# Attention over eight images: both output groups at the start of a pass, back to back

## The chip, the cores and the metric

The kernel runs on 1 core of one Trainium2 chip. The metric is device time in microseconds (us) of one execution. The engines are named as the profile names them: PE (TensorE, with PEld for its weight loads), DVE (VectorE), ACT (ScalarE), POOL (GpSimd) and SP (SyncE, which here issues DMAs).

## What is computed

The input x has 8 images of 768 channels and 32 x 32 = 1024 positions. It is normalised in 32 groups, goes through 12-head attention with head size 64, and is added back:

```python
def _L0_conv_ref(x, Wq, Wk, Wv, Wp):
    ...
    q = conv1x1(Wq)
    k = conv1x1(Wk)
    v = conv1x1(Wv)
    scale = 1.0 / jnp.sqrt(jnp.asarray(dh, dtype=x.dtype))
    scores = jnp.einsum('bhdn,bhdm->bhnm', q, k) * scale
    attn = jax.nn.softmax(scores, axis=-1)
    out = jnp.einsum('bhnm,bhdm->bhdn', attn, v)
    out = out.reshape(B, C, H, W)
    return jnp.einsum('oc,bchw->bohw', Wp, out)
...
x = x + _L0_conv_ref(_gn(x), L0_conv_Wq, L0_conv_Wk, L0_conv_Wv, L0_conv_Wp)
```

## The kernel before

A first phase (`project_phase`, about the first 1220 us) normalises x and writes q, k and v to DRAM. The change does not touch it. The second phase (`attend_phase`) is a chain of 48 **passes**, 0 to 47, one for each pair of heads: 6 passes make one image. Every engine runs its own program in order, and they meet only at semaphores, so the order in which each program is written out is the schedule.

A pass has 8 **steps** t (128 keys each). PE does in a step:

- `scores_by_key` (L873): the scores of pass p, 128 keys by 1024 queries for two heads, in two halves h. Each half is 8 matmuls in two PSUM banks. The first 6 are q times k, the last 2 (shown as `ones_r`) subtract each query's maximum, which lies in a row `top`. ACT turns each half into exponents (L988, tile `p_all`, a ring of three slots).
- `scores_by_query` (L855), called a **unit**: scores of the next pass, laid out so that DVE can take maxima (L1026). There are 16 units in a pass and one pair of banks for them, so a unit waits for the maximum of the unit before it.
- `values` (L886): exponents times v, for the step before. `values` of step 7 is done in the next pass.
- An **out group** (`output`, L896): 18 matmuls of the last projection for an earlier image, 128 channels by 512 positions, from tile `a`. From pass 8 on (`LAG` = 8) each pass has two, numbered 0 and 1; both write PSUM bank 7, and DVE adds x to the result (`add_x`, L1065).

The bank of an out group is also one of the banks of scores (`SCORE_BANKS = (0, 1, 2, 7)`, where the last two are half h = 1). So half 1 of a step waits for the `add_x` behind a group.

At the end of a pass DVE turns the maxima into rows (L93, L97, L99), and SP sends them with two DMAs to `top` (L87). POOL adds the exponents up over the steps (L830, 14 adds a pass), multiplies the heads of pass p - 2 by their reciprocal sums in step 1 (`divide`, L813), and in step 3 makes their low part (`low_out`, L818). SP stores the high and low parts to DRAM (L743, L745).

Tile `a` holds 6 blocks of those heads for half an image. SP **reloads** it in every third pass (10, 13, ..., 46, thirteen times): after the store of the low part has landed it issues six DMAs of 512 KB (L737), and out group 0 of the pass behind waits for each block in turn:

```python
                if begins:
                    sp.wait_ge(o_out, full - 32)
                    for kt in range(KT - 1 if p == LAG - 1 else 0, KT):
                        load_a((p - LAG) * 2 + 1, b - 1, 0 if j < SHIFT else 1, kt)
```

DVE also reduces the row sums of the pass before: a transpose and a sum for each head (L1038 `turn_sums`, L1043 `sum_rows`), then small steps (`gather_parts` L1050 in step 5, `add_parts` L1055 and `reciprocals` L1059 in step 6).

Of the kernel before, what the change touches and what calls it, by code (L numbers as in the profile page):

```python
# [19 lines left out]
def f32(ap):  # L20

    return ap.bitcast(F32)
# [62 lines left out]
def send_maxima(sp, shared, turned, e, MT, DH):  # L85
    for i in range(2):
        sp.dma_start(f32(shared.top[e][i * DH:i * DH + 1, :]).rearrange("a (t n) -> a t n", t=MT),  # L87
                     f32(turned[i * MT:(i + 1) * MT, :])).then_inc(shared.top_in, 16)
# [475 lines left out]
def attend_phase(nc, S, shared, x, q_dram, k_dram, v_dram, o_dram, recip_dram, out, psum):  # L564
# [9 lines left out]
    OUT_AT = (0, MT // 2)  # L574
    UNITS_BY_STEP = ((1, 1, 1, 0),) + ((0, 0, 1, 1),) * (MT - 2) + ((0, 0, 1, 0),)
    UNITS = 2 * MT
# [7 lines left out]
    small = psum[:, 7, :]  # L584
    half_of = (slice(0, DH), slice(DH, P))

    with ExitStack() as ctx:
# [94 lines left out]
        def units(t):  # L682

            done = sum(map(sum, UNITS_BY_STEP[:t]))
            ends = [done + sum(UNITS_BY_STEP[t][:n]) for n in range(5)]
            return [range(a, z) for a, z in zip(ends, ends[1:])]
# [8 lines left out]
        def _(sp):  # L695
# [9 lines left out]
            def maxima(p, m):  # L705

                sp.wait_ge(neg_done, p + 1)
                send_maxima(sp, shared, turned[m % 2], m % SLOTS, MT, DH)

            def spread_recip(p):  # L710
                wait(sp, o_done, p)
                sp.wait_ge(recip_done, p + 1)
                sp.dma_start(recip_dram.rearrange("i (c r) -> c i r", r=SQUARE), compact.rearrange("c (i r) -> c i r", i=2)).then_inc(recip_out, 16)
# [33 lines left out]
            def pair(p, m, b):  # L747
# [36 lines left out]
            store_group(NP - 1, 1, *where(B - 1, KT - 1, 1))  # L784
            load_x(NP, 1, *where(B, 0, 1))
# [6 lines left out]
            load_x(NP + 1, 0, *where(B, 1, 0))  # L792
            spread_recip(NP - 1)
# [49 lines left out]
        def _(pe):  # L843
# [57 lines left out]
            def pair(p, m, u):  # L901
# [6 lines left out]
                def group(s):  # L908
                    n = 2 * (m - LAG) + s
                    if s == 1:  # L910
                        pe.wait_ge(exp_done, (p * MT + OUT_AT[1] + 1) * 4)
                    wait(pe, y_done, (p - LAG) * 2 + s)
                    output(small, n % KT, PRODUCTS, (2 * (p - LAG) + s) // KT + 1 if u is None else u * (2 * BODY // KT) + (n // KT + 1))

                for t in range(MT):
                    front, behind, late, end = units(t)
                    maxima(front)
                    if t == 0:
                        if not first:
                            values(p - 1, m - 1, None, MT - 1)  # L920
                        if at_least(p, LAG):
                            group(0)
# [10 lines left out]
                    if t == OUT_AT[1] and at_least(p, LAG):  # L933
                        group(1)
# [43 lines left out]
        def _(act):  # L978
# [11 lines left out]

            def take_heads(p, m):
# [28 lines left out]
        def _(dve):  # L1020
# [40 lines left out]
            def add_x(n, s, count, bank=small):  # L1061
# [9 lines left out]
            def pair(p, m, u):  # L1071
                first, last = known(p) and p == 0, known(p) and p == NP - 1
                for t in range(MT):
                    front, behind, late, end = units(t) if not last else [()] * 4
                    for unit in front:
                        unit_max(p + 1, m + 1, unit)
                    if t == OUT_AT[0] and at_least(p, LAG):
                        add_x((p - LAG) * 2, 0, p - LAG + 1)
# [11 lines left out]
                    if t == OUT_AT[1] and at_least(p, LAG):  # L1090
                        add_x((p - LAG) * 2 + 1, 1, p - LAG + 1)
# [62 lines left out]
```

## Time and profile before

| what | value |
|---|---|
| median of 3 runs | 3353.2 us (3352.13 to 3356.67) |
| the profiled execution, its own time | 3353.56 us |
| its span in the trace | 3351.8 us |
| PE busy | 3318.9 us (99%) |
| DVE, ACT, POOL busy | 1779.8, 1088.7, 1837.7 us |
| mean granted TensorE clock | 0.998 |

The span is what the trace covers; the execution's own time is 1.76 us longer. Busy time of an engine is a share of the span. Since matmuls are pipelined, a PE that is "busy" can still be held up between two matmuls, so the steps between starts say more than the share.

### The profile page before, as it was taken

The page shows a single profiled execution, that of the slowest core. Times are in us where ns is not written, and L with a number is a line of the kernel's source. Part 1 is how long each engine was busy: PE and PEld are TensorE (multiplying, and loading weights), DVE is VectorE, ACT ScalarE, POOL GpSimd, SP SyncE. Part 2 cuts the span into 40 slices and gives each one's busy share as a digit, 9 for nine tenths or more (in the row PEclk, how much of TensorE's full clock was granted, in tenths as well). Part 3 has the DMA queues.
Part 4 walks back from the last instruction along what each step waited for, and adds up shares of the span by engine and source line. Part 5 has one row for each costly group of instructions (what it writes and reads, how often), then busy time and mean ns, then how long its engine had stood idle before and what let it go on. Part 6 is the DMA issues. An engine that isn't in the chain of part 4 may idle for free.

```text
span 3351.8 us, 47690 instructions
## 1 busy us (share of the span) xinstructions
PE 3318.9 (99%) x18286; PEld 2255.5 (67%) x18286; DVE 1779.8 (53%) x2377; ACT 1088.7 (32%) x1945; POOL 1837.7 (55%) x793
## 2 busy tenths in 40 slices
PE   8999999999999999999999999999999999999999
PEld 7888888888888865555555555555555555555557
DVE  6232323233233257776666666666666666666652
ACT  3111111111111124444444434444444444444441
POOL 2000000000000049999888888888888888888883
PEclk9999999999999999999999999999999999999999
DMA  7243433423243433233434434434344344343434
GB/s 244 102 142 107 145 136 119 146 101 138 103 149 112 155 107 120 108 136 133 161 126 156 150 119 144 152 131 164 120 164 156 125 151 137 124 159 133 157 102 170
DMA packets 222930, 461.57 MB, mean 138 GB/s; under 512 B 22944, under 2 KB 74784, under 8 KB 221856
## 3 DMA queue, kind: packets, MB, share of 16 engines
q1 hardware_dynamic: 222752, 459.16, 39.2%
q8 instruction: 116, 1.90, 0.2%
q14 instruction: 62, 0.51, 0.0%
HBM read 259.06 MB, written 199.62 MB: 137 GB/s over the span
## 4 chain that ended last, share of the span: by engine, by line
PE 55%; issue 3%; DMA 2%; ACT 1%; POOL 1%; DVE 1%; SPq 0%; ACTq 0%; POOLq 0%
PE psum L873 19%; PE psum L886 19%; PE psum L896 10%; PE psum L855 6%; PE psum L954 1%; ACT p_all L988 1%; DMA recip_rows<-compact 1%; POOL sums L830 1%; DMA w_second<-turned 1%; DVE half_max L1026 0%; DMA x_first<-turned 0%; SPq L87 0%; SPq L716 0%; DVE flipped L97 0%; DVE compact L1059 0%
## 5 line engine op out<-in xcount | busy, mean ns | idle before, releaser
L830 POOL TENSOR_TENSOR sums<-sums,p_all 128x1024 f32<-128x1024 f32 x576 | 1353.1, 2392 | 0.0
L1026 DVE TENSOR_REDUCE half_max<-psum 128x2 f32<-128x1024 f32 x752 | 921.4, 1225 | 493.1 <-PE psum L855 487.3
L988 ACT ACTIVATE p_all<-psum 128x512 f32<-128x512 f32 x1536 | 793.0, 602 | 948.4 <-PE psum L873 943.9
L886 PE MATMUL psum<-p_all,v 128*64 128x512 f32 x3072 | 743.4, 605 | 0.0
L438 POOL MEMSET x_first<- 128x1024 f32 x1 | 1.0, 955 | 1074.1 <-PE psum L352 1074.1
L873 PE MATMUL psum<-w_second 64*128 64x512 f32 x3072 | 448.0, 396 | 13.3 <-DMA w_second<-turned 6.4
L414 ACT CAST stage<-psum 128x512 fp32r<-128x512 f32 x192 | 112.9, 588 | 963.3 <-PE psum L352 948.0
L886 PEld LDWEIGHTS psum<-p_all,v 128*64 128x64 f32 x3072 | 186.3, 136 | 352.0 <-issue 248.3
L532 DVE TENSOR_TENSOR stage<-psum,stage 128x512 fp32r<-128x512 f32 x192 | 132.7, 692 | 528.5 <-ACT stage L414 528.5
L830 POOL TENSOR_TENSOR sums<-p_all 128x1024 f32<-128x1024 f32 x96 | 226.7, 2385 | 306.8 <-ACT p_all L988 306.8
L896 PE MATMUL psum<-a,w_first 128*128 128x512 f32 x1512 | 367.5, 397 | 0.0
L896 PEld LDWEIGHTS psum<-a,w_first 128*128 128x128 f32 x1512 | 277.5, 188 | 121.5 <-issue 33.3
L873 PEld LDWEIGHTS psum<-w_second 64*128 64x128 f32 x3072 | 286.2, 185 | 90.4 <-ACT p_all L988 27.3
L855 PE MATMUL psum<-w_second 64*128 64x512 f32 x1024 | 230.0, 444 | 2.5 <-PEq L118 2.0
L855 PEld LDWEIGHTS psum<-w_second 64*128 64x128 f32 x1024 | 96.4, 184 | 198.6 <-DVE half_max L1026 141.1
L873 PE MATMUL psum<-x_first 64*128 64x512 f32 x1536 | 223.3, 395 | 4.1 <-DMA x_first<-turned 2.6
L537 DVE COPY stage<-psum 128x384 f32<-128x384 f32 x128 | 71.4, 557 | 251.7 <-PE psum L352 251.7
L352 PE MATMUL psum<-w_third,x_second 128*128 128x384 f32 x1152 | 203.2, 335 | 0.0
L352 PE MATMUL psum<-w_third,x_first 128*128 128x384 f32 x1152 | 202.8, 335 | 0.0
L873 PE MATMUL psum<-x_first,ones_r 64*128 64x512 f32 x1024 | 202.4, 390 | 0.0
L352 PEld LDWEIGHTS psum<-w_third,x_second 128*128 128x128 f32 x1152 | 199.7, 188 | 2.5 <-issue 2.0
L352 PEld LDWEIGHTS psum<-w_third,x_first 128*128 128x128 f32 x1152 | 199.8, 188 | 0.6
(96 smaller groups left out, 3267.5 us busy)
## 6 DMA issues: line engine op xcount, KB each, us to landing
q_parts<-stage SPq DMA_DIRECT2D x192, 256.0 KB, 2.2
k_parts<-stage SPq DMA_DIRECT2D x192, 256.0 KB, 2.3
a<-o_parts SPq DMA_DIRECT2D x84, 512.0 KB, 7.7
w_second<-q_parts SPq DMA_DIRECT2D x32, 1024.0 KB, 5.1
w_second<-k_parts SPq DMA_DIRECT2D x32, 1024.0 KB, 7.6
v_rows<-stage SPq DMA_DIRECT2D x128, 192.0 KB, 2.1
v<-v_rows SPq DMA_DIRECT2D x48, 512.0 KB, 4.5
stage<-recip_rows SPq DMA_DIRECT2D x96, 256.0 KB, 3.8
```

What stands on the lines that cost most here:

```text
L352: mm = pe.matmul(out, lhs, rhs, start=(kt == 0 and n == 0), stop=(kt == KT - 1 and n == 2))
L414: act.copy(stage[:, r, 0:BANK], psum[:, r, :]).then_inc(hi_done, 1)
L532: dve.tensor_tensor(stage[:, r, BANK:2 * BANK], psum[:, r, :], f32(stage[:, r, 0:BANK]), ALU.subtract).then_inc(lo_done, 1)
L537: dve.tensor_copy(f32(stage[:, r, 0:VC]), psum[:, r, 0:VC]).then_inc(lo_done, 1)
L830: pool.tensor_tensor(sums[:, m % 2, i, :], first, p_all[:, i, n, :], ALU.add).then_inc(added, 1)
L855: mm = pe.matmul(rows[:, i, :], queries, k[e][part, 0, h * BANK:(h + 1) * BANK], start=True, stop=True)
L873: mm = pe.matmul(psum[:, SCORE_BANKS[2 * h + i], :], left, right, start=(c == 0), stop=(c == 3))
L886: mm = pe.matmul(heads[part, h, :], v[:, e, t, part], p_all[:, i, (m * MT + t) % EXPS, cols], start=(t == 0), stop=(t == MT - 1))
L896: mm = pe.matmul(bank, wp[:, wpart, kt, ot * P:(ot + 1) * P], a_of[kt][:, apart, :], start=first, stop=final)
L954: mm = pe.matmul(psum[:, LAST_BANKS[n], :], wp[:, wpart, kt, ot * P:(ot + 1) * P], a_last[kt][:, apart, half * BANK:(half + 1) * BANK], st ...
L988: act.activation(p_all[:, i, (m * MT + t) % EXPS, h * BANK:(h + 1) * BANK], psum[:, SCORE_BANKS[2 * h + i], :], ACT.Exp, scale=SCALE).then ...
L1026: dve.tensor_reduce(half_max[:, :, t, h], rows, AX.X, ALU.max, negate=True).then_inc(max_done, 1)
```

## The change

Both out groups of a pass stand at its start, ahead of everything else, one behind the other. Group 0 writes bank 7 and group 1 bank 2, both banks of scores half 1. `values` of the step 7 before, and ACT's copy of the heads (`take_heads`), move behind the scores and exponents of step 0. The 16 units are spread a little differently over step 0. DVE's row sums no longer stand as one block in step 4 but between units in steps 2 to 5, in all passes. SP stores and reloads both x tiles at one place, behind the load of v; it stores the reciprocals, sends one maximum row and then spreads the reciprocals, and ACT sends the other row. The wait for `top` stands ahead of the last matmul pair of the first scores in all passes.

```diff
     UNITS_BY_STEP = ((1, 1, 1, 0),) + ((0, 0, 1, 1),) * (MT - 2) + ((0, 0, 1, 0),)
+    UNITS_WITH_OUT = ((1, 0, 1, 1),) + UNITS_BY_STEP[1:]
...
-    small = psum[:, 7, :]
+    out_banks = (psum[:, 7, :], psum[:, 2, :])
...
@@ SP: maxima, spread_recip
-                send_maxima(sp, shared, turned[m % 2], m % SLOTS, MT, DH)
+                send_maxima(sp, shared, turned[m % 2], m % SLOTS, MT, DH, (0,))
+
+            def store_recip(p):
+                sp.wait_ge(recip_done, p + 1)
+                sp.dma_start(recip_dram.rearrange("i (c r) -> c i r", r=SQUARE), compact.rearrange("c (i r) -> c i r", i=2)).then_inc(recip_out, 16)
...
@@ SP: pair
-                if at_least(p, LAG + 1):
-                    store_group(p - 1, 1, *where(b, j - 1, 1) if j else where(b - 1, KT - 1, 1))
-                if at_least(p, LAG):
-                    load_x(p, 1, *where(b, j, 1))
...
-                if at_least(p, LAG):
-                    store_group(p, 0, *where(b, j, 0))
-                if at_least(p, LAG - 1):
-                    load_x(p + 1, 0, *where(b, j + 1, 0) if j < KT - 1 else where(b + 1, 0, 0))
+                for s in range(2):
+                    if at_least(p, LAG):
+                        store_group(p, s, *where(b, j, s))
+                    if at_least(p, LAG - 1):
+                        load_x(p + 1, s, *where(b, j + 1, s) if j < KT - 1 else where(b + 1, 0, s))
...
                 if at_least(p, 1):
-                    spread_recip(p - 1)
+                    store_recip(p - 1)
                 if not (known(p) and p == NP - 1):
                     maxima(p + 1, m + 1)
+                if at_least(p, 1):
+                    spread_recip(p - 1)
...
@@ PE: scores_by_key, pair
-                top_at = (0, 0, 3 if p == 0 else 0)
+                top_at = (0, 0, 3)
...
-                if h == 1 and t in (OUT_AT[0], OUT_AT[1] + 1) and at_least(p, LAG):
-                    pe.wait_ge(y_done, (p - LAG) * 2 + (1 if t == OUT_AT[0] else 2))
+                if h == 1 and t == 0 and at_least(p, LAG):
+                    pe.wait_ge(y_done, (p - LAG) * 2 + 2)
...
-                    front, behind, late, end = units(t)
+                    front, behind, late, end = units(p, t)
+                    if t == 0 and at_least(p, LAG):
+                        group(0)
+                        group(1)
                     maxima(front)
-                    if t == 0:
-                        if not first:
-                            values(p - 1, m - 1, None, MT - 1)
-                        if at_least(p, LAG):
-                            group(0)
+                    if t == 0 and not first and before(p, LAG):
+                        values(p - 1, m - 1, None, MT - 1)
...
                     if t > 0:
                         values(p, m, u, t - 1)
-                    if t == OUT_AT[1] and at_least(p, LAG):
-                        group(1)
+                    elif at_least(p, LAG):
+                        values(p - 1, m - 1, None, MT - 1)
                     maxima(end)
...
@@ ACT: pair
-                    if t == 0 and not first:
+                    if t == 0 and not first and before(p, LAG):
                         take_heads(p - 1, m - 1)
                     exponent(p, m, t, 0)
                     exponent(p, m, t, 1)
+                    if t == MT - 1 and not (known(p) and p == NP - 1):
+                        second_maxima(p + 1, m + 1)
+                    if t == 0 and at_least(p, LAG):
+                        take_heads(p - 1, m - 1)
...
@@ DVE: pair
                         for n in range(4):
-                            if t == (OUT_AT[1] if at_least(p, LAG) else n + 1):
+                            if t == n + 2:
```

The engines' orders show where work now stands. First PE, at the start of pass 17 of the kernel before (L855 units, L873 scores, L886 values, L896 an out group; the first row, `values` of step 6, still belongs to pass 16):

```order
1138 L886 MATMUL psum<-p_all,v 64x512 x4
1139 L855 MATMUL psum<-x_first 128x512 x2
1140 L886 MATMUL psum<-p_all,v 64x512 x4
1141 L896 MATMUL psum<-a,w_first 128x512 x18
1142 L855 MATMUL psum<-x_first 128x512 x2
1143 L873 MATMUL psum<-w_second 128x512 x6
```

The start of pass 17 of the changed kernel, where the lines are L856, L874, L887 and L897:

```order
1129 L887 MATMUL psum<-p_all,v 64x512 x4
1130 L897 MATMUL psum<-a,w_first 128x512 x36
1131 L856 MATMUL psum<-x_first 128x512 x2
1132 L874 MATMUL psum<-w_second 128x512 x6
1133 L874 MATMUL psum<-w_second,ones_r 128x512 x2
1134 L874 MATMUL psum<-w_second 128x512 x6
1135 L874 MATMUL psum<-w_second,ones_r 128x512 x2
1136 L856 MATMUL psum<-x_first 128x512 x2
1137 L887 MATMUL psum<-p_all,v 64x512 x4
1138 L856 MATMUL psum<-x_first 128x512 x2
```

The 36 matmuls of both groups come straight behind `values` of step 6; one unit and `values` of step 7 now stand behind them and the first scores.

Second DVE, in pass 21 of the kernel before, around its step 4 (L1026 a unit's maximum, L1038 and L1043 the row sums, L1065 `add_x`, L1050 `gather_parts`):

```order
730 L1026 TENSOR_REDUCE half_max<-psum 128x2 x9
731 L1038 STREAM_TRANSPOSE flip<-sums 128x1024
732 L1043 TENSOR_REDUCE part<-flip 128x32
733 L1038 STREAM_TRANSPOSE flip<-sums 128x1024
734 L1043 TENSOR_REDUCE part<-flip 128x32
735 L1065 TENSOR_TENSOR stage<-psum,stage 128x512
736 L1026 TENSOR_REDUCE half_max<-psum 128x2 x2
737 L1050 STREAM_TRANSPOSE quads<-part 32x64 x2
738 L1026 TENSOR_REDUCE half_max<-psum 128x2
```

The same work in pass 21 of the changed kernel, steps 2 to 5, with the lines L1034, L1046, L1051 and L1058:

```order
723 L1046 STREAM_TRANSPOSE flip<-sums 128x1024
724 L1034 TENSOR_REDUCE half_max<-psum 128x2 x2
725 L1051 TENSOR_REDUCE part<-flip 128x32
726 L1034 TENSOR_REDUCE half_max<-psum 128x2 x2
727 L1046 STREAM_TRANSPOSE flip<-sums 128x1024
728 L1034 TENSOR_REDUCE half_max<-psum 128x2 x2
729 L1051 TENSOR_REDUCE part<-flip 128x32
730 L1058 STREAM_TRANSPOSE quads<-part 32x64 x2
731 L1034 TENSOR_REDUCE half_max<-psum 128x2
```

Each of the four large operations stands alone between two maxima, except the last: it meets the first half of `gather_parts` (row 730) ahead of the same maximum.

## Rows read from the trace of the kernel before

**Rows 1.** Stretches: us; busy PE, PEld, DVE, ACT, POOL; clock; DMA share; GB/s.
```profile
1370.00:1374.00 4.00, 4.00 (x24) 3.85 (x24) 0.69 (x1) 2.17 (x4) 4.00 (x3) 0.59 1.02 414
1376.44:1526.20 149.76, 145.52 (x908) 76.21 (x906) 108.28 (x129) 72.48 (x134) 149.75 (x64) 1.00 0.38 136
1900.00:2300.00 400.00, 398.65 (x2357) 225.39 (x2358) 260.98 (x309) 166.44 (x307) 339.84 (x146) 1.00 0.42 144
```

**Rows 2.** Timeline of PE, start of pass 19: start, busy, line, tile, count.
```profile
2002.63 0.50 PE L855 MATMUL psum<-w_second 64*128 64x512 f32 x2
2003.06 1.94 PE L886 MATMUL psum<-p_all,v 128*64 128x512 f32 x8
2004.93 4.38 PE L896 MATMUL psum<-a,w_first 128*128 128x512 f32 x18
2009.23 0.50 PE L855 MATMUL psum<-w_second 64*128 64x512 f32 x2
2009.57 0.86 PE L873 MATMUL psum<-w_second 64*128 64x512 f32 x6
...
2011.42 0.39 PE L855 MATMUL psum<-w_second 64*128 64x512 f32 x2
2011.91 0.97 PE L873 MATMUL psum<-w_second 64*128 64x512 f32 x6
...
2013.92 0.39 PE L855 MATMUL psum<-w_second 64*128 64x512 f32 x2
...
2016.11 0.51 PE L855 MATMUL psum<-w_second 64*128 64x512 f32 x2
```

**Rows 3.** PE timeline: pass 19's second out group, then four groups after pass 47.
```profile
2029.25 4.42 PE L896 MATMUL psum<-a,w_first 128*128 128x512 f32 x18
...
3282.95 16.61 PE L896 MATMUL psum<-a,w_first 128*128 128x512 f32 x72
3299.40 1.52 PE L954 MATMUL psum<-x_first,w_first 128*128 128x512 f32 x6
```

**Rows 4.** PE timeline, passes 5 and 7: units, and one that waited for DVE.
```profile
1425.52 0.39 PE L855 MATMUL psum<-x_first 64*128 64x512 f32 x2
...
1488.76 0.50 PE L855 MATMUL psum<-w_second 64*128 64x512 f32 x2
...
1491.15 0.50 PE L855 MATMUL psum<-w_second 64*128 64x512 f32 x2
1491.59 0.65 PE L886 MATMUL psum<-p_all,v 128*64 128x512 f32 x2
```

**Rows 5.** DVE timeline: a row sum between maxima (pass 5), then gathering (pass 19).
```profile
1427.09 1.21 DVE L1043 TENSOR_REDUCE part<-flip 128x32 f32<-128x1024 f32 x1
1428.25 1.23 DVE L1026 TENSOR_REDUCE half_max<-psum 128x2 f32<-128x1024 f32 x1
...
2037.35 0.48 DVE L1050 STREAM_TRANSPOSE quads<-part 32x64 f32<-32x64 f32 x2
```

**Rows 6.** POOL timeline, pass 19: the first adds, and the low part.
```profile
2014.94 4.72 POOL L830 TENSOR_TENSOR sums<-p_all 128x1024 f32<-128x1024 f32 x2 [6.59 <-ACT p_all L988]
...
2031.33 2.42 POOL L818 TENSOR_TENSOR o_lo<-stage,o_hi 128x1024 fp32r<-128x1024 f32 x1
```

**Rows 7.** The reload in pass 19: SP's issues, and time to landing.
```profile
L737 SPq DMA_DIRECT2D a<-o_parts x6: 371/586/983, 2036.6 to 2039.8; - x6
...
DMA to landing us min/median/max: 5.5/7.5/8.9
```

**Rows 8.** The same for the reload in pass 10.
```profile
L737 SPq DMA_DIRECT2D a<-o_parts x6: 371/468/979, 1637.3 to 1640.2; - x6
...
DMA to landing us min/median/max: 4.9/7.2/9.9
```

**Rows 9.** PE timeline: out group behind pass 19's reload; pass 47's first scores, with their wait.
```profile
2049.03 4.38 PE L896 MATMUL psum<-a,w_first 128*128 128x512 f32 x18
...
3246.58 0.97 PE L873 MATMUL psum<-w_second 64*128 64x512 f32 x6 [1.29 <-DMA w_second<-turned]
```

More of the change, by code:

```diff
@@ L82, in load_pair, with send_maxima @@
     sp.dma_start(f32(shared.k[e]), k_dram[:, ch, :].rearrange("s p n -> p s n")).then_inc(shared.qk_in[e], 16)
[L85 to L88, printed above, removed]
+def send_maxima(eng, shared, turned, e, MT, DH, heads=range(2)):
+    for i in heads:
+        eng.dma_start(f32(shared.top[e][i * DH:i * DH + 1, :]).rearrange("a (t n) -> a t n", t=MT),
+                      f32(turned[i * MT:(i + 1) * MT, :])).then_inc(shared.top_in, 16)
 def turn_maxima(dve, shared, p, neg_max, flipped, turned, half_max, MT):
@@ L573, in attend_phase @@
     SCALE = float(DH) ** -0.5
-    OUT_AT = (0, MT // 2)
     UNITS_BY_STEP = ((1, 1, 1, 0),) + ((0, 0, 1, 1),) * (MT - 2) + ((0, 0, 1, 0),)
+    UNITS_WITH_OUT = ((1, 0, 1, 1),) + UNITS_BY_STEP[1:]
     UNITS = 2 * MT
@@ L680, in after, with units @@
             return (p + 1, m + 1, u)
-        def units(t):
-            done = sum(map(sum, UNITS_BY_STEP[:t]))
-            ends = [done + sum(UNITS_BY_STEP[t][:n]) for n in range(5)]
+        def units(p, t):
+            steps = UNITS_WITH_OUT if at_least(p, LAG) else UNITS_BY_STEP
+            done = sum(map(sum, steps[:t]))
+            ends = [done + sum(steps[t][:n]) for n in range(5)]
             return [range(a, z) for a, z in zip(ends, ends[1:])]
@@ L707, in maxima @@
                 sp.wait_ge(neg_done, p + 1)
-                send_maxima(sp, shared, turned[m % 2], m % SLOTS, MT, DH)
+                send_maxima(sp, shared, turned[m % 2], m % SLOTS, MT, DH, (0,))
+            def store_recip(p):
+                sp.wait_ge(recip_done, p + 1)
+                sp.dma_start(recip_dram.rearrange("i (c r) -> c i r", r=SQUARE), compact.rearrange("c (i r) -> c i r", i=2)).then_inc(recip_out, 16)
             def spread_recip(p):
                 wait(sp, o_done, p)
-                sp.wait_ge(recip_done, p + 1)
-                sp.dma_start(recip_dram.rearrange("i (c r) -> c i r", r=SQUARE), compact.rearrange("c (i r) -> c i r", i=2)).then_inc(recip_out, 16)
                 sp.wait_ge(recip_out, 16 * (p + 1))
@@ L782, in _ @@
                 pair(p, p % BODY, p // KT)
-            store_group(NP - 1, 1, *where(B - 1, KT - 1, 1))
-            load_x(NP, 1, *where(B, 0, 1))
             sp.wait_ge(s_ready, NP * MT * 4)
@@ L792, in _ @@
             load_x(NP + 1, 0, *where(B, 1, 0))
+            store_recip(NP - 1)
             spread_recip(NP - 1)
@@ L909, in group @@
                     n = 2 * (m - LAG) + s
[L910 to L913, printed above, removed]
+                    pe.wait_ge(exp_done, p * MT * 4)
+                    wait(pe, y_done, (p - LAG) * 2)
+                    output(out_banks[s], n % KT, PRODUCTS, (2 * (p - LAG) + s) // KT + 1 if u is None else u * (2 * BODY // KT) + (n // KT + 1))
                 for t in range(MT):
-                    front, behind, late, end = units(t)
+                    front, behind, late, end = units(p, t)
+                    if t == 0 and at_least(p, LAG):
+                        group(0)
+                        group(1)
                     maxima(front)
-                    if t == 0:
-                        if not first:
-                            values(p - 1, m - 1, None, MT - 1)
-                        if at_least(p, LAG):
-                            group(0)
+                    if t == 0 and not first and before(p, LAG):
+                        values(p - 1, m - 1, None, MT - 1)
                     if first and t == 0:
@@ L989, in exponent, with second_maxima @@
                                    scale=SCALE).then_inc(exp_done, 1)
+            def second_maxima(p, m):
+                act.wait_ge(neg_done, p + 1)
+                send_maxima(act, shared, turned[m % 2], m % SLOTS, MT, DH, (1,))
             def take_heads(p, m):
@@ L1059, in reciprocals, with add_x @@
                 dve.reciprocal(compact[:], compact[:]).then_inc(recip_done, 1)
-            def add_x(n, s, count, bank=small):
+            def add_x(n, s, count, bank):
                 dve.wait_ge(kt_done, (n + 1) * KT)
@@ L1073, in pair @@
                 for t in range(MT):
-                    front, behind, late, end = units(t) if not last else [()] * 4
+                    front, behind, late, end = units(p, t) if not last else [()] * 4
+                    if t == 0 and at_least(p, LAG):
+                        for s in range(2):
+                            add_x((p - LAG) * 2 + s, s, p - LAG + 1, out_banks[s])
                     for unit in front:
                         unit_max(p + 1, m + 1, unit)
-                    if t == OUT_AT[0] and at_least(p, LAG):
-                        add_x((p - LAG) * 2, 0, p - LAG + 1)
                     for unit in (*behind, *late):
@@ L1089, in pair @@
                                     sum_rows(p - 1, n // 2)
-                    if t == OUT_AT[1] and at_least(p, LAG):
-                        add_x((p - LAG) * 2 + 1, 1, p - LAG + 1)
                     if t == FINISH_AT and not first:
```

## Prediction

> **What bounds the kernel now.** I read the busy time by stretch first. From 1900 to 2300 us PE is busy for 398.65 of 400 us at full clock; DVE, ACT and POOL are busy for 261, 166 and 340 [rows 1]. So from pass 8 on PE sets the pace, and time can only come from gaps between its matmuls, which the timeline shows by steps between starts. It can be lost wherever something that PE waits for comes later than PE. From 1376 to 1526 us (passes 4 to 7, no out groups) POOL is busy for 149.75 of 149.76 us [rows 1]: there POOL sets the pace, and a gap that PE loses is worth little.
>
> **Part 1: PE's order in passes 8 to 46.** Pass 19 shows the pieces [rows 2]. Unit 0 takes 0.43 us (2002.63 to 2003.06), `values` 1.87, out group 0 4.30, the unit behind it 0.34, both halves of scores 1.85 (2009.57 to 2011.42). Unit 2 then takes 0.49, since the scores behind it wait for exponents, the scores of step 1 2.01, and unit 3 with `values` 2.19, that is 0.32 for the unit. From unit 0 to unit 3 that is 11.29 us. The second group is as long: 4.42 busy [rows 3] against 4.38, so 4.34 by starts. Together 15.63.
>
> After, the same work is: both groups, unit, scores, unit, `values`, unit, scores. Four groups in a row take 3299.40 - 3282.95 = 16.45 us for 72 matmuls [rows 3], that is 0.228 each or 4.11 a group, where a lone group takes 4.30. With one change of shape at the end, 0.15, two take 8.38. The rest: 0.34 + 1.85 + 0.32 + 1.87 + 0.34 + 1.85 = 6.57, with nothing waiting for exponents, because `values` now lies between the two steps' scores. 14.95 in all, a gain of 0.68 us a pass. Bounds: 0.3 if the exponents' wait stays, 0.8 if the second group costs 4.08. Over 39 passes: **-26.5**.
>
> The scores' half 1 waits for both `add_x`. The last one stands where it stood, 1.27 us behind the end of a group, ahead of the same work; I count nothing. If DVE were late there by 0.3 us, it would cost 12 us in all (a rival below). ACT's `take_heads` goes into the 2.2 us in which ACT waits for the next scores, and its DMA issue into its idle time during the out groups; the load of v moves behind `values` of step 7 but is used a pass later.
>
> **Part 2: DVE's row sums.** In step 5 DVE must now do, from one unit's maximum to the next: maximum, `sum_rows`, two small transposes, maximum. In pass 5 the unit at 1425.52 has its row sum start at 1427.09, 1.57 us behind it [rows 4, 5]. Add 1.21 (sum), 0.48 (transposes), 1.23 (maximum) [rows 5] and two hand-overs of 0.03: the second maximum ends 4.55 us behind the first unit's start. PE wants to start the unit after these two at 2.19 + 2.20 = 4.39 [rows 2]. So it is 0.16 late, plus some 0.05 for the release. A unit that waited for DVE shows what such a wait adds: in pass 7 it started 2.39 instead of 2.19 behind its forerunner, and then took 0.44 instead of 0.32 [rows 4], since its weights were not loaded ahead. I take 0.16 + 0.05 + 0.12 = 0.32 rounded down; ends 0 and 0.5. The other three row sums stand alone between maxima: a row sum delays the next maximum by 1.16 us [rows 5], which leaves 0.2 us or more. In passes 1 to 7 POOL hides the same stall. 39 passes: **+12.5**. Before, all four operations were covered by the 4.3 us of the second out group.
>
> **Part 3: the reload of `a`.** It starts when the low part of the heads has been stored, and POOL makes that part at a fixed place in its chain of adds. POOL starts a pass's chain when the exponents of step 1 are there: in pass 19 at 2014.94, having waited 6.59 us for ACT [rows 6]. Those exponents follow the scores of step 1, which end 11.29 us behind the start of pass 19, and 14.95 after the change (part 1). So POOL's chain, the low part (ended at 2033.75 [rows 6]) and the first issue of the reload (2036.6 [rows 7]) all come 3.66 us later in the pass. SP is not held up elsewhere by then: both stores and loads of x start behind `values` of step 7 and are over long before.
>
> What needs the reload comes sooner. Before, out group 0 began at 2049.03 [rows 9], 12.43 us behind the first issue; the thirteen reloads, read in the same way, give 12.0 to 12.6. Now it starts ahead of unit 0 and `values`, 2.30 us sooner, and the pass before it is 0.68 - 0.32 = 0.36 shorter. With the 3.66, the distance falls by 6.32 to 6.1, and typically 6.2. The group reaches its sixth block 3.6 us later, at 9.8. The sixth block lands 3.2 + 8.9 = 12.1 us behind the first issue in one case [rows 7], 2.9 + 9.9 = 12.8 in another [rows 8]; the thirteen lie between 11.7 and 13.0, with a mean of 12.4. Before, it was needed at 16.1, so nothing showed. Now PE waits for it 2.6 us, spread over the blocks, and 0.2 for weights not loaded ahead: 2.8 in each of 13 passes, **+36.4**. Bounds: 1.8, if the six blocks land as fast as the quickest (11.7), and 5, if the reciprocals' rows and the next q and k, now issued while the blocks still land, get in their way.
>
> **Part 4: the ends.** Passes 2 to 7: the wait for the maximum rows (as the 1.29 in pass 47 [rows 9]) goes, because one issue is saved and three matmul pairs come ahead of the wait. But POOL's chain is full, so only what PE gains in the passes before it filled up counts: **-3** (0 to -6). Pass 47 has no units and loses its 1.29 as well; without a group in its middle POOL holds step 7's exponents up for about half a us: **-1.5**.
>
> **Sum.** -26.5 + 12.5 + 36.4 - 3 - 1.5 = +17.9, on the profiled execution's 3353.56: 3371.5. The median of the runs is 0.4 lower, within the spread; I leave it at 3371.5.
>
> **A rule against the change.** The stalls of part 3 are gaps in PE's work. In this trace the clock fell at the start of pass 4, behind a wait of PE: over 1370 to 1374 us it was granted 0.59 of full speed [rows 1], the 1.2 GHz level for most of it, which costs 0.41 x 4 = 1.6 us. Other such waits did not bring it down, as the 1.29 us in pass 47 [rows 9]: the mean clock of the span is 0.998. The Trainium skill, in TensorE: Matmul & The Clock Gate (section Why this matters for your kernels), says that idle gaps between bursts of matmuls send the clock back. By the page the sum could be that of rival B; as the trace has it, a fall is the exception, and I leave it out of the sum.
>
> **The rivals.**
> A, faster: the reload is hidden after all. For that the blocks must land by 9.8 us behind the first issue, or the issue must not move. Speaks for it: the first block lands after 4.9 to 5.5 us, ahead of its need. Against: all the sixth ones took 11.7 or more. It decides at a distance of 8.6 us where I find 6.2. Time: 3371.5 - 36.4 = 3335.
> B, slower than forecast: each reload's gaps also cost the clock, or another 1.6 us by transfers in their way: 13 x 1.6 = 21, 3392.
> C: DVE's step 5 is not late, because the operations overlap more than counted (0.16 us decides): 3371.5 - 12.5 = 3359.
> D: `add_x` of both groups in a row comes late for half 1, or the second adds wait: 0.3 to 0.6 in 40 passes, 12 to 24: 3389.
>
> **How the numbers follow.** Forecast 0.52 (its own range 3363 to 3381); A 0.10; B 0.14; C 0.12; D 0.08; others 0.04. A measurement of this kernel tells 0.2%, 6.7 us, from no change. Faster: A and half of the others, 0.12. Same: C, mostly, 0.11. Slower: forecast, B, D and the rest, 0.77. The range leaves out A and the far end of B: 3357 to 3393.
>
> **What would show it.** PE's timeline: two groups of 8.4 us, no wait for exponents behind the first scores, the unit of step 6 some 0.3 us late behind DVE. In passes 11, 14, ..., 47 the first group takes about 7 us instead of 4.3, its matmuls waiting for DMA `a<-o_parts`; the first issue of a reload lies some 6 us ahead of the group instead of 12.5. All other passes should be about 43.8 us instead of 44.1. I am wrong if the first group of these passes runs through, or if a pass without a reload is no shorter.

## The result and the profile after

The changed kernel takes 3364.33 us (median of 7 runs, 3362.51 to 3366.5), the kernel before 3352.98 us in the runs beside it. The ratio is 1.0034 with a 95% interval of 1.0023 to 1.0044: 11.4 us slower. The profiled execution took 3363.46 us, with a span of 3361.7 us.

The busy shares of the two pages look alike (PE 3318.1 us, 99% of the span); the gaps are what differs. First the same stretch as in [rows 1], by engine: PE is busy 3.1 us less in 400 us.

```profile
1900.00:2300.00 400.00, 395.53 (x2338) 223.52 (x2336) 254.10 (x306) 165.43 (x305) 336.74 (x145) 1.00 0.42 143
```

The start of pass 19 in PE's timeline answers to [rows 2] and [rows 3]:

```profile
1999.96 8.46 PE L897 MATMUL psum<-a,w_first 128*128 128x512 f32 x36
2008.35 0.50 PE L856 MATMUL psum<-w_second 64*128 64x512 f32 x2
2008.68 0.86 PE L874 MATMUL psum<-w_second 64*128 64x512 f32 x6
...
2010.54 0.39 PE L856 MATMUL psum<-w_second 64*128 64x512 f32 x2
2010.86 1.94 PE L887 MATMUL psum<-p_all,v 128*64 128x512 f32 x8
...
2013.06 0.86 PE L874 MATMUL psum<-w_second 64*128 64x512 f32 x6
...
2014.90 0.39 PE L856 MATMUL psum<-w_second 64*128 64x512 f32 x2
```

From the groups to unit 3 it takes 2014.90 - 1999.96 = 14.94 us, where 14.95 was forecast. Both groups take 8.39, and no scores wait for exponents (0.33 us from the unit at 2012.73 to the scores at 2013.06). That was the gain. The loss shows where pass 20 begins, behind the reload of pass 19, once more in PE's timeline:

```profile
2043.61 1.66 PE L897 MATMUL psum<-a,w_first 128*128 128x512 f32 x6
2045.57 0.96 PE L897 MATMUL psum<-a,w_first 128*128 128x512 f32 x3 [0.30 <-DMA a<-o_parts]
2046.89 0.96 PE L897 MATMUL psum<-a,w_first 128*128 128x512 f32 x3 [0.36 <-DMA a<-o_parts]
2048.24 0.96 PE L897 MATMUL psum<-a,w_first 128*128 128x512 f32 x3 [0.39 <-DMA a<-o_parts]
2049.52 5.06 PE L897 MATMUL psum<-a,w_first 128*128 128x512 f32 x21 [0.32 <-DMA a<-o_parts]
2054.51 0.50 PE L856 MATMUL psum<-x_first 64*128 64x512 f32 x2
```

Three matmuls, a wait for the next block, three matmuls: both groups take 10.90 us (2054.51 - 2043.61) instead of 8.39. The bracket shows only what is left of each wait when the last matmul's modelled end is subtracted; the distance between the starts, about 1.3 us for work of 0.69, shows it whole. POOL's and SP's timelines and the landings of this reload, which answer to [rows 6] and [rows 7]:

```profile
2015.99 4.74 POOL L831 TENSOR_TENSOR sums<-p_all 128x1024 f32<-128x1024 f32 x2 [6.10 <-ACT p_all L988]
```

```profile
2037.42 3.85 SPq L740 DMA_DIRECT2D a<-o_parts  x6
```

```profile
DMA to landing us min/median/max: 5.2/7.6/9.1
```

The first issue, at 2037.42, lies 6.19 us ahead of the group (12.43 before), and the transfers themselves are about as fast as before: the sixth block lands 11.6 to 13.4 us behind the first issue, 12.2 on average (11.6 to 13.1 and 12.4 before). Over the whole span the waits, grouped by who waited for whom, have two rows that the kernel before does not have:

```profile
PEld psum L897 <- DMA a<-o_parts: 44.7, 55, 1.6
PE psum L897 <- DMA a<-o_parts: 21.0, 49, 1.2
```

They overlap, since a late weight load makes its matmul late too, so they are not added up. Where the time went is read from the starts of the first out group of each pass:

| part of the span | before | after | difference |
|---|---|---|---|
| first unit to first group of pass 8 | 297.91 | 292.29 | -5.6 (2.3 of it work now behind the group) |
| 26 passes without a reload before them, mean | 44.09 | 43.67 | 26 x -0.42 = -11.0 |
| 12 passes behind a reload (11 to 44), mean | 44.45 | 46.61 | 12 x 2.15 = +25.9 |
| pass 46 | 43.49 | 43.66 | +0.2 |
| first group of pass 47 to the end | 110.9 | 113.4 | +2.5 |

Together +11.9 us. The spans differ by only 9.9, because the first unit came at 1217.68 us instead of 1219.72 in this execution; the change touches nothing ahead of it. Behind a reload the two groups take 2.9 us longer than elsewhere, as a mean of all 13 (2.1 to 4.2).

### The profile page after: what moved, and what is told of

Same layout as the page of the kernel before. It is cut to its first block, busy times and chain, and to the rows that moved or that the text cites. A ratio compares the mean times of both kernels' runs of the same rounds, so it can differ in the third digit from the quotient of the medians.

```text
span 3361.7 us, 47629 instructions
## 1 busy us (share of the span) xinstructions
PE 3318.1 (99%) x18286; PEld 2251.0 (67%) x18286; DVE 1766.2 (53%) x2377; ACT 1087.8 (32%) x1945; POOL 1839.2 (55%) x793
## 4 chain that ended last, share of the span: by engine, by line
PE 47%; issue 7%; DMA 5%; POOL 3%; SPq 1%; ACT 1%; DVE 0%; POOLq 0%; ACTq 0%; DVEq 0%
PE psum L874 15%; PE psum L887 15%; PE psum L897 9%; PE psum L856 6%; DMA a<-o_parts 4%; POOL sums L831 2%; PE psum L954 1%; DMA o_parts<-o_lo 1%; SPq L740 1%; ACT p_all L988 1%; POOL o_lo L819 1%; POOL stage L814 0%; DVE half_max L1034 0%; DMA x_first<-turned 0%; DVE flipped L97 0%
## 5 line engine op out<-in xcount | busy, mean ns | idle before, releaser
L1034 DVE TENSOR_REDUCE half_max<-psum 128x2 f32<-128x1024 f32 x752 | 918.7, 1222 | 394.0 <-PE psum L856 389.0
L887 PE MATMUL psum<-p_all,v 128*64 128x512 f32 x3072 | 743.8, 605 | 0.1
L874 PE MATMUL psum<-w_second 64*128 64x512 f32 x3072 | 441.5, 392 | 3.6 <-ACT p_all L988 3.2
L887 PEld LDWEIGHTS psum<-p_all,v 128*64 128x64 f32 x3072 | 186.1, 136 | 351.8 <-issue 239.2
L897 PE MATMUL psum<-a,w_first 128*128 128x512 f32 x1512 | 371.9, 398 | 21.2 <-DMA a<-o_parts 21.0
L897 PEld LDWEIGHTS psum<-a,w_first 128*128 128x128 f32 x1512 | 277.3, 188 | 131.9 <-DMA a<-o_parts 44.7
L874 PEld LDWEIGHTS psum<-w_second 64*128 64x128 f32 x3072 | 287.5, 184 | 69.3 <-ACT p_all L988 14.4
L856 PEld LDWEIGHTS psum<-w_second 64*128 64x128 f32 x1024 | 96.0, 184 | 219.5 <-DVE half_max L1034 194.0
L856 PE MATMUL psum<-w_second 64*128 64x512 f32 x1024 | 233.3, 450 | 2.4 <-PEq L118 2.0
L1073 DVE TENSOR_TENSOR stage<-psum,stage 128x512 f32<-128x512 f32 x84 | 58.0, 691 | 324.8 <-PE psum L897 313.3
L874 PE MATMUL psum<-x_first 64*128 64x512 f32 x1536 | 221.3, 393 | 2.2 <-ACT p_all L988 2.0
L874 PE MATMUL psum<-x_first,ones_r 64*128 64x512 f32 x1024 | 201.5, 389 | 0.7 <-DMA x_first<-turned 0.7
```

The source lines that it names most:

```text
L856: mm = pe.matmul(rows[:, i, :], queries, k[e][part, 0, h * BANK:(h + 1) * BANK], start=True, stop=True)
L874: mm = pe.matmul(psum[:, SCORE_BANKS[2 * h + i], :], left, right, start=(c == 0), stop=(c == 3))
L887: mm = pe.matmul(heads[part, h, :], v[:, e, t, part], p_all[:, i, (m * MT + t) % EXPS, cols], start=(t == 0), stop=(t == MT - 1))
L897: mm = pe.matmul(bank, wp[:, wpart, kt, ot * P:(ot + 1) * P], a_of[kt][:, apart, :], start=first, stop=final)
L1034: dve.tensor_reduce(half_max[:, :, t, h], rows, AX.X, ALU.max, negate=True).then_inc(max_done, 1)
L1073: dve.tensor_tensor(y[:, s, :], bank, y[:, s, :], ALU.add).then_inc(y_done, 1)
```

## Experiments

Ten kernels ran. Ratios are to the kernel before on the same chip. Its median there was 3354.0 to 3354.4 us, against 3352.98 beside the changed kernel, so a difference of 1 to 2 us between times of two experiments says nothing.

**1. The reload early.** Only one of the six blocks, and only in every second reload, depends on the heads stored in the same pass. The edit loads the others first:

```diff
+                begins = j in (SHIFT - 1, SHIFT + KT // 2 - 1) and at_least(p, LAG - 1)
+                ready = KT - 1 if j < SHIFT else KT
+                if begins and p > LAG - 1:
+                    sp.wait_ge(o_out, full - 64)
+                    for kt in range(ready):
+                        load_a((p - LAG) * 2 + 1, b - 1, 0 if j < SHIFT else 1, kt)
                 if at_least(p, 2):
                     store_head(p - 2)
-                begins = j in (SHIFT - 1, SHIFT + KT // 2 - 1) and at_least(p, LAG - 1)
-                if begins:
+                if begins and ready < KT:
                     sp.wait_ge(o_out, full - 32)
-                    for kt in range(KT - 1 if p == LAG - 1 else 0, KT):
-                        load_a((p - LAG) * 2 + 1, b - 1, 0 if j < SHIFT else 1, kt)
+                    load_a((p - LAG) * 2 + 1, b - 1, 0, KT - 1)
```

> The changed kernel, but SP loads the blocks of a that depend on nothing recent ahead of the store of the heads (all six in passes 10, 16, ..., 46, five of six in passes 13, 19, ..., 43; the sixth stays behind the store). Theory: the first out groups of passes 11, 14, ..., 47 lose 2.9 us each (13 x 2.9 = 37.6) to the landing of these blocks and to nothing else. Then the time is 3364.3 - 37.6 = 3327, 26 us below the kernel before, all of these groups take 8.1 to 8.5 us, and no wait for a<-o_parts is left. Rival 1: the time is given back to another wait as soon as this one is gone (POOL's chain, the rows of maxima): 3345 or more. Rival 2: the earlier transfers collide with the loads of x and the stores of the heads, and make those late: no gain, 3360 or more.

Measured: 3326.68 us, ratio 0.9915 (0.990 to 0.993). Passes behind a reload take 43.67 us on average, like the others, and no wait for `a<-o_parts` is left. SP's timeline in pass 19 shows both parts of the reload:

```profile
2012.96 3.18 SPq L740 DMA_DIRECT2D a<-o_parts  x5
2016.19 0.79 SPq L746 DMA_DIRECT2D o_parts<-o_hi  x1
2026.28 0.33 SPq L748 DMA_DIRECT2D o_parts<-o_lo  x1
2028.92 0.37 SPq L740 DMA_DIRECT2D a<-o_parts  x1
```

The 37.7 us are those of the theory. The late reload is the whole reason why the change is slower, and both rivals fall: nothing else takes its place.

**2. The row sums a step earlier.** One line of DVE's program in the changed kernel:

```diff
-                            if t == n + 2:
+                            if t == n + 1:
```

> The changed kernel, but the four large operations on the row sums stand in steps 1 to 4 instead of 2 to 5, so that the last one no longer meets the first half of the gathering in step 5. Theory: that meeting delays the unit of step 6 by 0.23 us in each of 39 passes: 3364.3 - 9 = 3355, and the unit behind step 5's scores is on time. Rival 1: the delay hides elsewhere: 3364, no change. Rival 2: the transpose in step 1 comes before POOL has finished the sums of the pass before, DVE waits and PE behind it: 3366 or more.

Measured: 3359.48 us, ratio 1.0015 (1.0006 to 1.0024), some 5 us under the changed kernel and not 9. DVE's timeline of the changed kernel shows the meeting in step 5 of pass 19, and PE's what it costs:

```profile
2034.01 1.21 DVE L1051 TENSOR_REDUCE part<-flip 128x32 f32<-128x1024 f32 x1
2035.25 0.50 DVE L1058 STREAM_TRANSPOSE quads<-part 32x64 f32<-32x64 f32 x2
2035.69 1.18 DVE L1034 TENSOR_REDUCE half_max<-psum 128x2 f32<-128x1024 f32 x1
```

```profile
2034.62 0.50 PE L856 MATMUL psum<-w_second 64*128 64x512 f32 x2
...
2036.92 0.50 PE L856 MATMUL psum<-w_second 64*128 64x512 f32 x2
2037.35 0.65 PE L887 MATMUL psum<-p_all,v 128*64 128x512 f32 x2
```

The maximum ends at 2036.87 and the unit starts at 2036.92, 2.30 us behind the one before, and takes 0.43 to the next start. In the experiment's trace the same unit is free:

```profile
2036.55 0.39 PE L856 MATMUL psum<-w_second 64*128 64x512 f32 x2
2036.87 1.94 PE L887 MATMUL psum<-p_all,v 128*64 128x512 f32 x8
```

It takes 0.32 to the next start. A pass without a reload before it became 0.19 us shorter (43.48 against 43.67). Passes behind a reload did not (46.66 against 46.61). The blocks land when they land, and a pass that gets to them sooner waits longer: what the pass with the reload gains, the pass behind it loses. So the mechanism holds, and the gain is 26 x 0.19 = 4.9 us and not 39 x 0.23.

**3. The row sums in one block**, in step 4 from pass 8 on as in the kernel before, with all else as changed:

```diff
-                            if t == n + 2:
+                            if t == (MT // 2 if at_least(p, LAG) else n + 2):
```

> The changed kernel, but with the row sums in one block in step 4 from pass 8 on, as in the kernel before, where the second out group stood beside them. Theory: four operations take 5.0 us of DVE in a row, and the second unit behind them comes 3.3 us late instead of 0.2: 39 x 3.2 = 125, 3489. So the second out group cannot leave step 4 without the spreading. Rival: PE finds the time again behind the block, as exponents and maxima of later steps run ahead: under 1 us a pass, below 3400.

Measured: 3540.29 us, ratio 1.0552 (1.0533 to 1.0571), 176 us over the changed kernel. PE's timeline, then clock and busy time of two stretches (columns as in [rows 1]):

```profile
2081.42 0.50 PE L856 MATMUL psum<-w_second 64*128 64x512 f32 x2
...
2087.08 0.50 PE L856 MATMUL psum<-w_second 64*128 64x512 f32 x2 [3.32 <-DVE half_max L1034]
2087.52 3.39 PE L887 MATMUL psum<-p_all,v 128*64 128x512 f32 x8
2090.84 0.68 PE L856 MATMUL psum<-w_second 64*128 64x512 f32 x2
```

```profile
2081.00:2087.00 6.00, 2.76 (x22) 1.62 (x18) 5.83 (x5) 2.07 (x4) 6.00 (x4) 1.00 0.05 20
2087.00:2090.80 3.80, 3.72 (x10) 0.87 (x10) 1.63 (x4) 0.00 (x0) 3.80 (x3) 0.61 0.52 164
```

The unit comes 5.66 - 2.19 = 3.47 us late, near the 3.3 expected. What was not expected stands in the clock column of the second stretch: behind this wait the granted clock falls, from 2.4 towards 1.2 GHz (0.61 as a mean), and unit and `values`, 2.19 us at full clock, take 3.76. That is 1.57 more. It happens in each of the 39 passes, and some pay more than the one shown: passes take 48.5 to 50.0 us, 49.13 on average, against 43.67. Of these 5.46 us 3.47 are the wait, and the other 2.0, by subtraction, go with the clock. The expected 3489 missed this term, and one that goes the other way: with passes this long the reload is hidden again (the two groups behind one take 8.4 us), so 37.7 us come back. 39 x 5.46 - 37.7 = 175, against 176 measured. Spreading the row sums is a condition of the change: the second out group had been their cover.

**4. The kernel before with an early reload**, its blocks issued between the stores of the high and the low part:

```diff
                 sp.dma_start(o_dram[0, ch, :], f32(o_hi[:])).then_inc(o_out, 16)
+                if between is not None:
+                    between()
                 sp.wait_ge(o_lo_done, p + 1)
...
+                if early:
+                    sp.wait_ge(o_out, full - 64)
                 if at_least(p, 2):
-                    store_head(p - 2)
...
+                    store_head(p - 2, ahead if early else None)
```

> The kernel before, with the same blocks of a loaded between the stores of the high and the low part. Its trace has passes behind a reload of 44.45 us on average against 44.09 for the others, with a wait for the rows of maxima, whose DMAs are issued behind the reload. Theory: these rows land late because the reload's transfers are ahead of them; with the reload 3 us or more earlier 13 x 0.36 = 4.7 us go: 3348.5. Rival: the rows are late for another reason (the next q and k, the reciprocals): no change, 3353.

Measured: 3346.69 us, ratio 0.9975 (0.9965 to 0.9985). Passes behind a reload fell from 44.45 to 44.10 us, and pass 47 with the tail, behind the thirteenth reload, by 1.3 us, more than the 0.36 counted for it. This wait of the kernel before, here at the start of pass 17, is gone:

```profile
1921.29 0.95 PE L873 MATMUL psum<-w_second 64*128 64x512 f32 x6 [0.45 <-DMA w_second<-turned]
```

The result fits the theory's sum, but SP's timeline in the kernel before, in pass 16, shows a different way from the reload to the rows:

```profile
1911.65 0.33 SPq L713 DMA_DIRECT2D recip_rows<-compact  x1
1916.40 1.16 SPq L716 DMA_DIRECT2D stage<-recip_rows  x2
1917.60 1.39 SPq L87 DMA_DIRECT2D w_second<-turned  x2
```

SP stores the reciprocals (L713, 8 KB) and waits for this store to land before it spreads them (L716) and then sends the rows (L87). The store took 4.7 us here; in all 13 passes with a reload 3.7 to 5.1, 4.4 on average, and 1.4 in the 24 others from pass 11 on. So the rows were not slow, they were issued late: on average 1.3 us behind the start of the next pass's out group 0 instead of 1.3 us ahead of it. In experiment 4 the store takes 2.0 us on average, and the rows go out 0.9 us ahead. The rival named the reciprocals as a reason apart from the reload; they are the link between the two.

**5. Both edits in the changed kernel**, those of experiments 1 and 2.

> The changed kernel with both edits: the early reload and the row sums in steps 1 to 4. With late row sums alone undone, only the passes without a reload became shorter (43.48 against 43.67 us), and the time fell by 5, not 9: what a pass with a reload gains it waits longer for the blocks. Theory: with the reload early, all 39 passes keep the 0.2 us: 3326.7 - 8 = 3319. Rival: the 0.2 us were only moved, and the two edits do not add up: 3326 or more.

Measured: 3318.43 us (3317.76 to 3319.63), ratio 0.9897 (0.9882 to 0.9912): 35 us faster than the kernel before. All passes take 43.45 us (43.67 in experiment 1), and the two edits add up. Pass 20 begins without a wait:

```profile
2031.62 8.47 PE L901 MATMUL psum<-a,w_first 128*128 128x512 f32 x36
2040.02 0.50 PE L860 MATMUL psum<-x_first 64*128 64x512 f32 x2
2040.36 0.86 PE L878 MATMUL psum<-w_second 64*128 64x512 f32 x6
...
2041.29 0.86 PE L878 MATMUL psum<-w_second 64*128 64x512 f32 x6
...
2042.22 0.40 PE L860 MATMUL psum<-x_first 64*128 64x512 f32 x2
2042.54 1.94 PE L891 MATMUL psum<-p_all,v 128*64 128x512 f32 x8
```

**6. The early reload in 7 of 13 passes**, those where no block depends on a fresh store: in experiment 1's edit the first condition becomes

```diff
-                if begins and p > LAG - 1:
+                if begins and j > SHIFT:
```

with all six blocks, and the other reloads stay where they were.

> The changed kernel, with the early reload only in passes 10, 16, ..., 46 (7 of 13), where no block depends on the head just stored. Theory: the cost lies in each reload by itself, so 7 x 2.9 = 20 us go: 3344, with groups of 8.1 us behind these and of 11 us behind the others. Rival: SP's order in one pass acts on the following ones, and the gain is not in proportion.

Measured: 3343.79 us, ratio 0.9971 (0.996 to 0.9982), as the theory has it. Each reload costs by itself.

**7. The kernel before with the late wait for the rows of maxima**, one edit of the change by itself:

```diff
-                top_at = (0, 0, 3 if p == 0 else 0)
+                top_at = (0, 0, 3)
```

> The kernel before, with the wait for the rows of maxima ahead of the last matmul pair of the first scores in all passes (one edit of the change alone). Theory: it takes 0.7 us off each such wait: all of the 0.4 us in passes behind a reload (12 x 0.36), 0.7 of the 1.3 in pass 47, and up to 0.7 in passes 1 and 2, while POOL holds passes 3 to 7: 3353 - 4.3 - 0.7 - 2 = 3346. Rival: the rows land so late that the last pair waits as long: 3352 or more.

Measured: 3345.24 us, ratio 0.9974 (0.9965 to 0.9983). In its trace passes behind a reload take 44.11 us instead of 44.45, pass 47 and the tail 1.4 us less, and pass 8 is reached 2.4 us sooner. Of all edits this one paid in the kernel as it stood.

**8. The changed kernel with the rows of maxima as before**: experiment 7's edit undone, and both rows sent by SP.

```diff
-                top_at = (0, 0, 3)
+                top_at = (0, 0, 3 if p == 0 else 0)
...
-                send_maxima(sp, shared, turned[m % 2], m % SLOTS, MT, DH, (0,))
+                send_maxima(sp, shared, turned[m % 2], m % SLOTS, MT, DH)
...
-                    if t == MT - 1 and not (known(p) and p == NP - 1):
-                        second_maxima(p + 1, m + 1)
```

> The changed kernel, with the rows of maxima as before: SP sends both, and all of the first scores wait for them. Theory: from pass 8 on they land during the out groups and cost nothing; the 3 us gained ahead of pass 8 come from them and go again: 3364.3 + 3 = 3367, and pass 8 starts some 3 us later in the trace. Rival: the gain ahead of pass 8 is that of the row sums' place, or chance: 3364.

Measured: 3369.89 us (3365.53 to 3370.99), ratio 1.0047 (1.0033 to 1.006). Pass 8 is reached 2.1 us later and passes without a reload keep their length (43.68 us), as the theory has it. The remaining excess of some 3 us lies in three passes of this execution (14, 32 and 47), in which the sixth block landed 1.0 to 1.3 us later than in the changed kernel's trace and the clock fell, so the size is less sure than the sign.

**9. `values` ahead again**, in the kernel of experiment 5: `values` of step 7 directly behind the out groups, the units of step 0 as before.

```diff
-    UNITS_WITH_OUT = ((1, 0, 1, 1),) + UNITS_BY_STEP[1:]
+    UNITS_WITH_OUT = UNITS_BY_STEP
...
-                    if t == 0 and not first and before(p, LAG):
+                    if t == 0 and not first:
                         values(p - 1, m - 1, None, MT - 1)
...
-                    elif at_least(p, LAG):
-                        values(p - 1, m - 1, None, MT - 1)
```

> The kernel of the run with both edits (early reload, row sums in steps 1 to 4), but values of step 7 and the units of step 0 stand as before: directly behind the out groups, ahead of the first scores. So the first scores of step 1 wait for exponents again. Theory: of the 0.64 us by which a pass became shorter, 0.42 come from this place (unit between two values 0.09, unit and scores behind exponents 0.33) and the rest from the two groups standing in a row: 43.45 + 0.42 = 43.87 a pass, 3318.4 + 40 x 0.42 = 3335. Rival: the wait is paid by the groups' place alone, 3320 or less.

Measured: 3335.91 us, ratio 0.9948 (0.9935 to 0.9962), and 43.86 us a pass instead of 43.45. Two thirds of what a pass gains come from `values` filling the time in which ACT makes the first exponents.

**10. The groups apart**, in the kernel of experiment 5: unit 0 stands between them.

```diff
                     if t == 0 and at_least(p, LAG):
                         group(0)
-                        group(1)
                     maxima(front)
+                    if t == 0 and at_least(p, LAG):
+                        group(1)
```

> The kernel of the run with both edits, but with unit 0 between the two out groups instead of behind them. Theory: two groups in a row save one change of shape, 0.22 to 0.3 us: 43.7 a pass, 3318.4 + 40 x 0.26 = 3329, with groups of 4.3 us to the next start and not 4.1. Rival: a lone group costs the same as one in a row, and only the places of the waits matter: 3319.

Measured: 3339.4 us, ratio 0.9957 (0.9943 to 0.997), 21 us over experiment 5, twice what was expected. PE's and DVE's timelines in pass 20:

```profile
2038.62 4.38 PE L901 MATMUL psum<-a,w_first 128*128 128x512 f32 x18
2042.93 0.50 PE L860 MATMUL psum<-x_first 64*128 64x512 f32 x2
2043.36 4.38 PE L901 MATMUL psum<-a,w_first 128*128 128x512 f32 x18
2047.67 0.96 PE L878 MATMUL psum<-w_second 64*128 64x512 f32 x6
...
2048.70 0.88 PE L878 MATMUL psum<-w_second 64*128 64x512 f32 x6
...
2049.66 0.50 PE L860 MATMUL psum<-x_first 64*128 64x512 f32 x2
2050.09 1.94 PE L891 MATMUL psum<-p_all,v 128*64 128x512 f32 x8
```

```profile
2047.78 0.69 DVE L1078 TENSOR_TENSOR stage<-psum,stage 128x512 f32<-128x512 f32 x1 [4.05 <-PE psum L901]
2048.39 1.22 DVE L1039 TENSOR_REDUCE half_max<-psum 128x2 f32<-128x1024 f32 x1
```

From the first group to `values` it takes 11.47 us, against 10.92 in experiment 5. The groups are 8.62 instead of 8.40, so a lone group does cost 0.11 more; the unit between them takes 0.43 instead of 0.34. The rest, 0.24 us, comes in two parts. The first half of the scores takes 1.03 us (2047.67 to 2048.70) where it takes 0.93 in experiment 5 (2040.36 to 2041.29): here these scores, and not a unit, are the first work of another shape behind group 1. And the next unit waits for DVE's maximum, which ends at 2049.61, so it takes 0.43 us instead of 0.32. This second part belongs to DVE's order: the experiment left it alone, and the maximum of unit 0 still stands behind both `add_x`, though the unit itself now stands ahead of group 1. So not all of the 21 us is the price of groups that stand apart.

## Why the prediction was right, and what was off

The way and the reason were as forecast; the size was 18 us where 11.4 were measured, inside the range. Parts 1 and 3, the two largest terms, came out close and with their mechanisms; the 6.5 us between 17.9 and 11.4 are smaller ones, named below.

**Part 1** (-0.68 a pass): 14.94 us against 14.95 where it was worked out. With DVE's delay removed, a pass takes 43.45 us instead of 44.09, 0.64 less. So the agreement to 0.01 at the start of the pass holds for those pieces alone, and the whole term was 0.04 too large. Experiment 9 gives 0.41 of it to the place of `values`, and the two groups of experiment 10 (8.62 against 8.40) give 0.22 to their standing in a row. Rival D, scores held up by `add_x`, did not come: both halves of the first scores take 1.86 us (2008.68 to 2010.54) against 1.85 before.

**Part 2** (+0.32 a pass): the mechanism was right, the size was 0.19 (experiment 2 against the changed kernel) to 0.21 (experiment 5 against 1, where no reload disturbs). The transposes and the maximum overlapped by a few hundredths each, so the unit came 0.11 late and not 0.2. Rival C, no delay at all, wanted an overlap of 0.16 us; there was 0.11.

**Part 3** (+36.4): 2.9 us for each of 13 reloads against 2.8. In pass 19, POOL's first add lies 16.03 us behind the pass's start instead of 12.31, 3.72 later (3.66 forecast), and the first issue 6.19 us ahead of the group (6.1 forecast for this pass). In 11 of the 13 reloads it is 6.2 us, in two 5.1 and 5.2. Experiment 1 took the whole 37.7 us back. Rival A, a hidden reload, is ruled out for this kernel; the distance that decides it is 6.2 + 2.6 = 8.8 us by the prediction's own terms, not the 8.6 it gives.

**Part 4** (-3 and -1.5): 3.3 us ahead of pass 8, of which the maxima's rows make most (2.4 in experiment 7, 2.1 in experiment 8). Pass 47 and the tail changed by 2.5 us, of which 1.9 are `values`, now behind the group, and 2.3 the thirteenth reload's wait; the rest is a gain of 1.7.

**The step that failed** is one of omission, in part 4: the wait for the rows of maxima was looked for at both ends of the chain of passes only. For the passes behind a reload it was put at nothing, without a reason. In the kernel before it stood there too, 0.36 us in 12 passes on average, because SP sent the rows late: it first waited for the reciprocals' store, which landed late behind the six blocks (experiment 4). The change removes this wait: 12 x 0.36 = 4.3 us more gain than forecast. Experiments 4 and 7 each removed it in the kernel before, one by an earlier reload, one by a later wait.

The table of starts gives the whole account, with the forecast in brackets: ahead of pass 8 -3.3 (-3), the 26 passes -11.0 (-9.4), the 12 passes behind a reload +25.9 (+29.3), from pass 46 on +0.4 (+0.9), once the 2.3 us of work that now stands behind the groups are moved across. Together +11.9 in these two traces, against +17.9. Most of the 6 us is the omitted wait; 39 passes shorter by 0.42 us instead of 0.36 (part 2 smaller than forecast by 0.11, part 1 by 0.04) make 2.3, the ends 0.5, and the reloads, at 2.9 us instead of 2.8, take 1.3 back.

**The rule on the clock** and rival B: one of the thirteen reloads did lose the clock, the one ahead of pass 35. Its mean clock was 0.65 over 4 us, as PE's timeline and the stretch show:

```profile
2714.52 0.97 PE L897 MATMUL psum<-a,w_first 128*128 128x512 f32 x3 [1.11 <-DMA a<-o_parts]
2716.15 8.05 PE L897 MATMUL psum<-a,w_first 128*128 128x512 f32 x27 [0.66 <-DMA a<-o_parts]
```

```profile
2715.00:2719.00 4.00, 3.34 (x10) 1.89 (x9) 0.00 (x0) 0.00 (x0) 4.00 (x2) 0.65 0.60 225
```

Pass 14 kept its clock (1.00 over 1776 to 1784 us) behind a first wait that was no shorter:

```profile
1777.86 0.96 PE L897 MATMUL psum<-a,w_first 128*128 128x512 f32 x3 [1.17 <-DMA a<-o_parts]
```

So the exception stayed an exception. Its price was small: the two groups of pass 35 took 12.55 us, 1.4 more than the mean behind the other twelve reloads, but 1.0 of this is the sixth block, which landed 7.2 us behind the group's start instead of 6.15. From that landing to the end of the groups it took 5.38 us against 5.03 to 5.05 in the other twelve, so 0.3 us is the clock's own; the slow matmuls ahead of it ran while PE had to wait anyway. Rival B had counted 1.6. Where the wait is long and whole, as in experiment 3, the clock falls in every pass, and nothing hides it; there the Trainium skill's warning, in TensorE: Matmul & The Clock Gate (section Why this matters for your kernels), about idle gaps between bursts of matmuls agrees with the trace. It is not told by these runs how the gaps' number and length weigh against each other.

## What to carry to other kernels

When work moves to an earlier place, look for the input that arrives just in time for the old place, and work out both shifts: in pass 19 the out groups came 2.7 us sooner and, through POOL's chain, the first issue of their blocks 3.5 us later. What was issued together with a late input need not be late itself: five or six of six blocks had been ready long before. Ask too what else stands behind a late transfer in the same program: the maxima's rows were late because SP waited for another store first. And a gain ahead of a fixed arrival is not a gain until the arrival is moved; the same edit was worth 5 us with the reload late and 8 us with it early.

## What the runs showed of the hardware that was not expected

A single wait of PE of 3.3 us brought the clock down in each of the 39 passes of experiment 3 (0.61 of full speed behind it in the pass shown) and cost 1.6 us more there, 2.0 on average. Gaps of up to 1.2 us between groups of three matmuls, 2.1 to 3.4 us of delay in sum, left it at 2.4 GHz in 12 of 13 reloads, and where it fell, most of the slow work lay inside the wait and only 0.3 us showed. A DMA of 8 KB issued behind six of 512 KB took 3.7 to 5.1 us to land instead of 1.4 in the kernel before; in the changed kernel, where it is issued sooner behind them, it took 7.8 to 9.0, but PE did not wait for it. In both it landed, on average, 0.2 us behind the last of the six blocks.
